# Causal masks of two query tiles as matmuls, VectorE's program as a loop, and side jobs in other steps: a cross-attention and expert-layer kernel

## The chip, the cores and the metric

The kernel runs on one core of a Trainium2 chip. The metric is the device time of one execution in microseconds (us), here the median of the runs shown; lower is better. The engines are TensorE (PE in profile rows; its weight loads are PEld), VectorE (DVE), ScalarE (ACT), GpSimd (POOL) and SyncE (SP), which issues most of the DMAs.

## The reference, cut to what matters

For 16 batches of 512 tokens with 256 features: 16-head attention (head size 16) against 1601 context tokens under a causal mask, then a layer in which 8 experts each pick 128 tokens of a batch.

```python
q = x @ Wq.T ; k = context @ Wk.T ; v = context @ Wv.T        # 16 heads of 16
scores = einsum('bhqd,bhkd->bhqk', q, k) * SCALE
causal = tril(ones((t, kv_t)))                                 # key <= query
scores = where(causal, scores, -inf)
probs = softmax(scores, axis=-1)
y = einsum('bhqk,bhkd->bhqd', probs, v) @ Wo.T + bo
x = x + tanh(g_xattn) * y
...
gating, idx = top_k(softmax(layernorm(x) @ gate_w.T), k)       # per expert, 128 of 512 tokens
x = x + tanh(g_ffn) * scatter_add(gating * (silu(h @ w_gate) * (h @ w_up)) @ w_down)
```

Because of the mask only the first 512 context tokens matter. A softmax row needs the maximum over the keys at or before its query, so the mask must act before the maximum is taken.

## The kernel before, in words

The kernel has two stages, `attention` and `experts`, one after the other. The change touches `attention` alone, and in it the part that runs once for each of the 16 batches.

**Steps.** The order of all work of a batch is written out by `steps(b)` (before: lines 81 to 126) and every engine's program walks the same list, taking from it what is its own. The list has 4 groups (of 4 heads) by 11 units `k`. Each of the 44 steps has a `("max", b, g, k)` piece, then, for `k < 10`, a `("sc", ...)` piece, then the side jobs that the table `extra[g][k]` puts there. A step is named (g, k) below.

**max.** `MAX_UNITS` cuts a group's 4 heads and 4 query tiles of 128 into 11 units: unit 0 is query tile 0 of four heads (4 matmuls of 128 columns), units 1 and 2 are tile 1 of two heads each (2 matmuls of 256 columns), units 3 to 6 are tile 2 and units 7 to 10 tile 3 of one head each (one matmul of 384 or 512 columns). A query tile needs only the keys up to its own, so a head's tiles have 128, 256, 384 and 512 columns. TensorE (line 453) writes the unresolved scores into one of three PSUM banks, up to two units ahead of VectorE (semaphore `max_read`). VectorE (line 681) then runs, for every head of the unit, one custom instruction that adds the mask tile `causal` and takes the row maximum, and reads the accumulator into `mx`. Its throw-away output goes to `masked`.

**sc.** TensorE computes the scores again, transposed and with minus the maximum added (lines 470 and 473; the fp32-accurate product is made from stacked bf16 parts), into one of two banks; ScalarE takes the exponential (line 565) and frees the bank (`exp_done`); GpSimd zeroes the masked diagonal blocks of `prob` (line 834).

**Side jobs.** `pv` multiplies probabilities with values (line 487, fp32, one piece for each key tile j, 4 a group) and ScalarE's `pv+` takes the result out; `yt`, `yt+` turn and normalise it; `mt`, `mt+` turn the maxima into a row (`m_sb`) and `mrow` sends it into the stacked operand `qs`; `q`, `k`, `v`, `o` are the projections (`q` and `k` are 12 matmuls of 512 columns each a batch, `v` and `o` 24 of 256 each), with `q+`, `k+`, `v+`, `o+` taking them out; `ln1`, `ln2` are layer-norm statistics on VectorE and `ln1+`, `ln2+` their application on ScalarE; `xt`, `ll`, `lt` make the expert logits; `xsplit`, `csplit`, `ysplit`, `xs` are bf16 splits on GpSimd; `qstore`, `kstore`, `qstack`, `kstack`, `xturn`, `cturn`, `yturn`, `load`, `res`, `save`, `mrow` are DMAs that SyncE issues in the list's order. Jobs that need a PSUM bank alternate between two (`JOB_BANK`). Side jobs belong to neighbouring batches (b - 2 to b + 2), so the stage is a software pipeline.

**Programs.** TensorE, ScalarE, GpSimd and SyncE run `rounds`: batches -1 to 2 written out, 3 to 13 as a hardware loop whose semaphore targets come from registers, 14 to 17 written out. VectorE runs `rounds_apart`, in which all 19 rounds are written out with constant targets:

```python
    def rounds_apart(body):
        for b in range(-1, BATCH + 2):
            for p in steps(b):
                body(b, p)
```

`wait_apart(eng, s, value, passed)` is a wait that, where its value is a register, is followed by an increment of the semaphore `passed`, so that it stays an instruction of its own.

Of the kernel before, what the change touches and what calls it, by code (L numbers as in the profile page):

```python
# [5 lines left out]
ALU = mybir.AluOpType  # L6
# [73 lines left out]
def steps(body):  # L80
# [7 lines left out]
        0: {0: [("pv", b - 1, 1, 0)],  # L88
            1: [("yt", b - 1, 0), ("pv", b - 1, 1, 1)],
            2: [("yt+", b - 1, 0), ("ln1+", b + 1, 0)],  # L90
            3: [("pv", b - 1, 1, 2), ("mrow", b - 1, 3), ("xsplit", b + 1, 0)],
            4: [("mt+", b - 1, 3), ("mt", b - 1, 3), ("ln1+", b + 1, 1)],
            5: [("pv", b - 1, 1, 3), ("o+", b - 2, 0), ("o", b - 2, 0, 0), ("o", b - 2, 0, 1), ("xsplit", b + 1, 1)],
            6: [("pv+", b - 1, 1), ("csplit", b + 1, 0), ("csplit", b + 1, 1)],
            7: [("o", b - 2, 1, 0), ("o", b - 2, 1, 1), ("o+", b - 2, 1), ("xturn", b + 1)],
            10: [("yt", b - 1, 1), ("qstack", b, 2), ("kstack", b, 2), ("cturn", b + 1)]},
        1: {1: [("mt", b, 0)], 2: [("yt+", b - 1, 1)],
            3: [("pv", b - 1, 2, 0), ("mt+", b, 0), ("ln2", b - 2, 0), ("ysplit", b - 1, 0)],
            4: [("q", b + 1, 0, 0), ("q", b + 1, 0, 1), ("q+", b + 1, 0)],
            5: [("pv", b - 1, 2, 1), ("ln2", b - 2, 1)],  # L100
            6: [("yturn", b - 1, 0), ("q", b + 1, 1, 0), ("q", b + 1, 1, 1), ("q+", b + 1, 1)],
            7: [("pv", b - 1, 2, 2)], 8: [("mrow", b, 0)],
            9: [("pv", b - 1, 2, 3), ("xs", b - 2), ("ln2+", b - 2, 1)],
            10: [("pv+", b - 1, 2), ("ln2+", b - 2, 0)]},
# [79 lines left out]
def attention(nc, ctx, stack, sb, sem, g):  # L184
# [103 lines left out]
    def rounds(eng, body):  # L288
# [7 lines left out]
        for b in range(BATCH - 2, BATCH + 2):  # L296
            for p in steps(b):
                body(b, p)

    def rounds_apart(body):  # L300

        for b in range(-1, BATCH + 2):
# [944 lines left out]
```

## Time and profile before

| | |
|---|---|
| runs | 1906.61, 1907.35, 1908.03 us; median 1907.35 us |
| profiled execution | 1905.62 us, of which the span from first to last instruction is 1903.9 us |
| busy, share of the span | PE 93%, PEld 53%, DVE 57%, ACT 49%, POOL 49% |
| instructions | 40685, of them PE 12902 matmuls, DVE 3480 busy ones |
| DMA | 247.85 MB, mean 130 GB/s |

Attention takes about the first 845 us. Between 120 and 720 us every 50 us look alike. The matmul durations of the profile are those of pipelined instructions: one lasts from its start until its result is out, and the next starts long before that. What a matmul costs TensorE in a stream is therefore the distance from its start to the next start, not its duration. Register, branch, semaphore and DMA-issuing instructions are not counted as busy.

### The profile page before, as it was taken

To read this page: it belongs to the slowest core of one execution; us is meant where nothing else is said; L and a number is where in the kernel's file an instruction comes from. 1 tells how busy PE (TensorE), PEld (TensorE's weight loads), DVE (VectorE), ACT (ScalarE), POOL (GpSimd) and SP (SyncE) were. 2 spreads that over 40 slices of the span, in tenths; PEclk is the share of its full clock that TensorE was granted. 3 is DMA by queue.
4 is the path that set the end of the run, shared out by engine and by line. 5 is a ranking of instruction groups with operands and counts; after the bars stand their busy time and mean duration, and the time that the engine had idled before them with its cause. 6 is when DMAs were issued, how large, how long until landed. Compare 5 with 4: busy or idle time off the path is not lost.

```text
span 1903.9 us, 40685 instructions
## 1 busy us (share of the span) xinstructions
PE 1772.4 (93%) x12902; PEld 1017.8 (53%) x12902; DVE 1079.0 (57%) x3480; ACT 930.5 (49%) x1812; POOL 931.3 (49%) x1026
## 2 busy tenths in 40 slices
PE   3899999999999999935899999999899999999997
PEld 1355555555555555422465656565556565656565
DVE  2778888888888887737634343434343434343431
ACT  2466666666666666632334343434343434343332
POOL 6477777777777776543333232333322323333322
PEclk8899999999999999967999999999999999999999
DMA  5777777777777787347464644556736555555222
GB/s 161 163 172 188 189 188 188 188 188 188 188 188 188 188 189 168 81 132 177 100 132 84 120 98 89 98 90 122 123 61 121 100 89 98 89 97 82 48 34 23
DMA packets 408333, 247.85 MB, mean 130 GB/s; under 512 B 289303, under 2 KB 389759, under 8 KB 408191
## 3 DMA queue, kind: packets, MB, share of 16 engines
q1 hardware_dynamic: 383183, 212.39, 47.7%
q0 software_dynamic: 24576, 33.57, 11.3%
q8 instruction: 72, 1.18, 0.3%
q14 instruction: 70, 0.57, 0.1%
q10 hardware_dynamic: 432, 0.13, 0.0%
HBM read 118.63 MB, written 58.72 MB: 93 GB/s over the span
## 4 chain that ended last, share of the span: by engine, by line
PE 50%; DVE 3%; DMA 1%; issue 1%; ACT 0%; POOL 0%; SPq 0%; POOLq 0%; DVEq 0%
PE bank L1101 11%; PE bank L1102 11%; PE bank L1103 11%; PE bank L1117 6%; PE bank L1119 6%; PE bank L1118 6%; DVE h L1219 0%; DVE h L1222 0%; DVE top_at L1169 0%; ACT h L1147 0%; DVE work L1172 0%; DVE top L1167 0%; DMA rows<-tokens,row_now 0%; DMA out<-y,row_now 0%; POOL out L1067 0%
## 5 line engine op out<-in xcount | busy, mean ns | idle before, releaser
L1067 POOL DMA_INDIRECT out<-y,row_now x128 | 202.5, 1582 | 606.6 <-ACT y L1154 581.7
L681 DVE CUSTOM_DVE_ANT_0 masked<-bank,causal 128x128 bf16<-128x128 f32 (+3 forms) x1024 | 445.6, 484 | 69.1 <-PE bank L453 68.2
L565 ACT ACTIVATE prob<-bank 128x512 f32<-128x512 f32 x640 | 367.6, 596 | 158.1 <-PE bank L473 86.1
L1219 DVE TENSOR_TENSOR h<-bank,silu 128x512 f32<-128x512 f32 x256 | 176.4, 689 | 393.5 <-PE bank L1103 259.8
L1147 ACT ACTIVATE h<-h 128x512 bf16<-128x512 f32 x256 | 161.2, 630 | 345.4 <-DVE h L1219 328.5
L1117 PE MATMUL bank<-downT,h 128*128 128x256 bf16 x1024 | 279.1, 273 | 0.0
L1119 PE MATMUL bank<-downT,h 128*128 128x256 bf16 x1024 | 279.1, 273 | 0.0
L1118 PE MATMUL bank<-downT,h 128*128 128x256 bf16 x1024 | 279.1, 273 | 0.0
L1222 DVE TENSOR_TENSOR h<-h 128x512 bf16<-128x512 f32 x256 | 177.3, 692 | 179.7 <-ACT h L1147 175.5
L453 PE MATMUL bank<-ks,qs 96*128 96x128 bf16 (+3 forms) x1024 | 257.8, 306 | 21.0 <-DMA ks<-k_parts 11.4
L1101 PE MATMUL bank<-tokT,gateT 128*128 128x512 bf16 x512 | 195.0, 381 | 35.7 <-DMA tokT<-rows 28.9
L470 PE MATMUL bank<-qs,ks 128*128 128x128 bf16 x1024 | 199.8, 221 | 12.8 <-ACT prob L565 11.5
L1101 PE MATMUL bank<-tokT,upT 128*128 128x512 bf16 x512 | 194.4, 380 | 6.7 <-DVE h L1219 6.6
L487 PE MATMUL bank<-prob,v_aug 128*32 128x512 f32 (+3 forms) x2048 | 193.1, 449 | 4.5 <-ACT yT L573 2.4
L473 PE MATMUL bank<-qs,ks 98*128 98x384 bf16 (+2 forms) x768 | 196.5, 273 | 0.0
L1103 PE MATMUL bank<-tokT,gateT 128*128 128x512 bf16 x512 | 195.1, 381 | 0.0
L1102 PE MATMUL bank<-tokT,gateT 128*128 128x512 bf16 x512 | 195.1, 381 | 0.0
L1102 PE MATMUL bank<-tokT,upT 128*128 128x512 bf16 x512 | 194.3, 380 | 0.0
L1103 PE MATMUL bank<-tokT,upT 128*128 128x512 bf16 x512 | 194.2, 379 | 0.0
L834 POOL TENSOR_SCALAR_AFFINE_SELECT prob<-prob 128x512 f32<-128x512 f32 x256 | 155.9, 635 | 72.8 <-ACT prob L565 72.7
L1154 ACT ACTIVATE y<-bank,gate_now 128x256 f32<-128x256 f32 x128 | 53.8, 471 | 260.1 <-PE bank L1119 260.1
L453 PEld LDWEIGHTS bank<-ks,qs 96*128 96x128 bf16 x1024 | 86.1, 98 | 168.1 <-DVE mx L681 80.3
(141 smaller groups left out, 2702.7 us busy)
## 6 DMA issues: line engine op xcount, KB each, us to landing
q_parts<-q_sb SPq DMA_DIRECT2D x64, 192.0 KB, 2.9
k_parts<-k_sb SPq DMA_DIRECT2D x64, 192.0 KB, 3.8
qs<-q_parts SPq DMA_DIRECT2D x64, 192.0 KB, 3.0
ks<-k_parts SPq DMA_DIRECT2D x64, 192.0 KB, 3.2
x_t<-in_x SPq DMA_DIRECT2D x16, 512.0 KB, 4.2
ctx_t<-in_ctx SPq DMA_DIRECT2D x16, 512.0 KB, 4.9
qs<-q_parts SPq DMA_DIRECT2D x64, 128.0 KB, 2.9
ks<-k_parts SPq DMA_DIRECT2D x64, 128.0 KB, 3.2
```

Of the source, the lines that this page charges most:

```text
L453: last = nc.tensor.matmul(dst[:, h * w:(h + 1) * w], qs[0:STACK, gr, h0 + h, i * P:(i + 1) * P], ks[0:STACK, gr, h0 + h, 0:w], start=True, ...
L470: last = nc.tensor.matmul(dst[:, at:at + P], ks[:, gr, h0 + h, j * P:(j + 1) * P], qs[:, gr, h0 + h, j * P:(j + 1) * P], start=True, stop= ...
L473: last = nc.tensor.matmul(dst[:, at + P:at + PWIDTH[j]], ks[0:ROWS, gr, h0 + h, j * P:(j + 1) * P], qs[0:ROWS, gr, h0 + h, (j + 1) * P:T], ...
L565: nc.scalar.activation(prob[:, gr % 2, h0:h0 + nh, POFF[tiles[0]]:POFF[tiles[0]] + w], sc_bank[SC_BANK[k]][:, 0:nh * w].rearrange("p (h w) ...
L681: last = nc.vector.tensor_tensor_reduce(masked[:, (gr * NMAX + k) % 2, part], max_bank[max_at(gr, k)][:, part], causal[:, T - w:T], 1.0, L ...
L1067: nc.gpsimd.indirect_dma_start(out_rows, bass.IndirectOffsetOnAxis(ap=row_now[:, par, c, s:s + 1], axis=0), y[:, c % 2, s, :], None, compu ...
L1101: nc.tensor.matmul(banks[it % 2][:, :], hi, xh, start=(dh == 0), stop=False)
L1102: nc.tensor.matmul(banks[it % 2][:, :], hi, xl, start=False, stop=False)
L1103: last = nc.tensor.matmul(banks[it % 2][:, :], lo, xh, start=False, stop=(dh == NH2 - 1))
L1117: nc.tensor.matmul(to, hh, wh, start=(it == 0), stop=False)
L1118: nc.tensor.matmul(to, hh, wl, start=False, stop=False)
L1119: last = nc.tensor.matmul(to, hl, wh, start=False, stop=(it == IT - 1))
```

## The change

Three things change in `attention`.

1. For units 0, 1 and 2 of each group (those with more than one head), each head's score matmul is followed by a second one that adds the mask to its last 128 columns, in the same accumulation: bf16 identity `identb` against the constant `mask_qk`. VectorE then takes the maxima of the whole unit with one plain `tensor_reduce` over a full bank, in place of 4 (unit 0) or 2 (units 1, 2) custom instructions with their accumulator reads. Units 3 to 10 stay as they were.
2. VectorE runs the same `rounds` as the other engines: batches 3 to 13 as a hardware loop.
3. The table `extra` is another one: the same 100-odd side jobs, in other steps and in another order within a step.

`identb` is cast once by VectorE; `mask_qk` is made once by GpSimd with a memset and an `affine_select` ahead of the others.

```diff
     extra = {
-        0: {0: [("pv", b - 1, 1, 0)],
-            1: [("yt", b - 1, 0), ("pv", b - 1, 1, 1)],
...
+        0: {0: [("mrow", b - 1, 3)],
+            1: [("ln1+", b + 1, 0), ("yt+", b - 1, 0), ("pv", b - 1, 1, 0), ("yt", b - 1, 0)],
...
@@ TensorE
                     for h in range(nh):
                         last = nc.tensor.matmul(
                             dst[:, h * w:(h + 1) * w], qs[0:STACK, gr, h0 + h, i * P:(i + 1) * P],
-                            ks[0:STACK, gr, h0 + h, 0:w], start=True, stop=True)
+                            ks[0:STACK, gr, h0 + h, 0:w], start=True, stop=nh == 1)
+                        if nh > 1:
+                            last = nc.tensor.matmul(dst[:, h * w + w - P:(h + 1) * w], identb[:, :], mask_qk[:, :],
+                                                    start=False, stop=True)
                     last.then_inc(max_filled, 1)
@@ VectorE
-                    wait(dve, max_read, n - 1)
-                    wait_apart(dve, max_filled, n + 1, passed["dve"])
-                    for h in range(nh):
-                        part = slice(h * w, (h + 1) * w)
-                        last = nc.vector.tensor_tensor_reduce(
-                            masked[:, (gr * NMAX + k) % 2, part], max_bank[max_at(gr, k)][:, part], causal[:, T - w:T], 1.0, LOWEST,
-                            ALU.add, ALU.max, mx[:, gr % 2, h0 + h, i:i + 1])
-                    last.then_inc(max_read, 1)
+                    if nh == 1:
+
+                        wait(dve, max_read, n - 1)
+                        wait_apart(dve, max_filled, n + 1, passed["dve"])
+                        nc.vector.tensor_tensor_reduce(
+                            masked[:, k % 2, 0:w], max_bank[max_at(gr, k)][:, 0:w], causal[:, T - w:T], 1.0, LOWEST,
+                            ALU.add, ALU.max, mx[:, gr % 2, h0, i:i + 1]).then_inc(max_read, 1)
+                        return
+                    wait(dve, max_filled, n + 1)
+                    nc.vector.tensor_reduce(mx[:, gr % 2, h0:h0 + nh, i], max_bank[max_at(gr, k)][
+                        :, 0:nh * w].rearrange("p (h w) -> p h w", h=nh), AX.X, ALU.max).then_inc(max_read, 1)
@@
-            rounds_apart(piece)
+            rounds(dve, piece)
@@ GpSimd, once
+            nc.gpsimd.memset(mask_qk[:, :], 0.0).then_inc(consts, 1)
...
+            nc.gpsimd.affine_select(out=mask_qk[:, :], in_=mask_qk[:, :], compare_op=ALU.is_ge, fill=NEG,
+                                    base=0, pattern=[[-1, P]], channel_multiplier=1).then_inc(consts, 1)
```

**TensorE, the first two units of a group.** First before, from a group's unit 0 to the second `sc` piece (L453 is a `max` matmul, L470 and L473 are `sc`):

```order
L453 MATMUL bank<-ks,qs 128x128 [waits max_read,stack_loaded3]
L453 MATMUL bank<-ks,qs 128x128 x3
L470 MATMUL bank<-qs,ks 128x128 [waits exp_done,mrow_loaded1]
L473 MATMUL bank<-qs,ks 128x384
L453 MATMUL bank<-ks,qs 128x256 [waits max_read]
L453 MATMUL bank<-ks,qs 128x256
L470 MATMUL bank<-qs,ks 128x128 [waits exp_done]
```

Now (L456 is the `max` matmul, L460 the mask's, L476 and L479 are `sc`), from the last head of unit 0 on:

```order
L456 MATMUL bank<-ks,qs 128x128
L460 MATMUL bank<-mask_qk,identb 128x128
L476 MATMUL bank<-qs,ks 128x128 [waits exp_done,mrow_loaded1]
L479 MATMUL bank<-qs,ks 128x384
L456 MATMUL bank<-ks,qs 128x256 [waits max_read]
L460 MATMUL bank<-mask_qk,identb 128x128
L456 MATMUL bank<-ks,qs 128x256
L460 MATMUL bank<-mask_qk,identb 128x128
L476 MATMUL bank<-qs,ks 128x128 [waits exp_done]
```

Each head of units 0 to 2 has its mask matmul behind it: 4 + 2 + 2 = 8 a group, 32 a batch, 512 in all, and each stands in front of the signal `max_filled`.

**VectorE, units 1 to 3 of a group.** Before, in the program written out, units 1 and 2 with the `yt+` behind them and unit 3:

```order
L681 ISA masked,mx<-bank,causal 128x256 [waits max_filled,max_read]
L681 ISA mx 128x1
L681 ISA masked,mx<-bank,causal 128x256
...
L704 RECIPROCAL rden<-bank 128x16 [waits yt_filled]
L708 TENSOR_TENSOR yq<-bank,rden 128x4x64 [waits y_lo_split,rden_done]
L681 ISA masked,mx<-bank,causal 128x384 [waits max_filled,max_read]
```

Now, in the loop's body (REGISTER_ALU and the ISA rows of L152 compute a semaphore target in a register), units 0 to 3:

```order
L152 ISA [waits mt_filled]
L692 TENSOR_REDUCE mx<-bank 128x4 [waits max_filled]
L152 REGISTER_ALU
L692 TENSOR_REDUCE mx<-bank 128x2 [waits max_filled]
L152 ISA
L713 RECIPROCAL rden<-bank 128x16 [waits yt_filled]
L152 ISA [waits rden_done]
L717 TENSOR_TENSOR yq<-bank,rden 128x4x64 [waits y_lo_split]
L152 REGISTER_ALU
L692 TENSOR_REDUCE mx<-bank 128x2 [waits max_filled]
L152 REGISTER_ALU [waits max_read]
L687 ISA masked,mx<-bank,causal 128x384 [waits max_filled]
```

Three reduces stand where eight custom instructions and eight accumulator reads stood; every wait of the loop has a register instruction before it; `yt+` of group 0 has moved from step (0, 2) to (0, 1).

**TensorE, two `pv` pieces side by side.** Before, `pv` of key tile 1 of group 1 stands in step (0, 1) and that of tile 2 in step (0, 3). Now both stand in step (0, 3), behind `mt` (L501), with only a register instruction between them:

```order
L152 ISA [waits v_read]
L501 MATMUL bank<-ident,mx 16x128 [waits max_read]
L152 REGISTER_ALU
L493 MATMUL bank<-prob,v_aug 32x384 [waits zeroed]
L493 MATMUL bank<-prob,v_aug 32x384 x3
L152 REGISTER_ALU
L493 MATMUL bank<-prob,v_aug 32x256 [waits zeroed]
```

The same happens with tiles 2 and 3 of group 0 in step (3, 10).

## Rows read from the trace of the kernel before

**Rows 1.** The page: busy time of the engines, and TensorE's granted clock in 40 slices.

```profile
PE 1772.4 (93%) x12902; PEld 1017.8 (53%) x12902; DVE 1079.0 (57%) x3480; ACT 930.5 (49%) x1812; POOL 931.3 (49%) x1026
PEclk8899999999999999967999999999999999999999
```

**Rows 2.** Busy time by window: us, each engine (instructions), clock, DMA share, GB/s.

```profile
219.00:696.30 477.30, 465.13 (x4211) 256.30 (x4210) 392.62 (x1691) 330.42 (x660) 363.00 (x461) 1.00 0.74 189
```

**Rows 3.** Timeline of PE, 365 to 376 us: start, duration, line, what, [idle before].

```profile
365.63 0.38 PE L453 MATMUL bank<-ks,qs 96*128 96x512 bf16 x1
365.84 0.22 PE L470 MATMUL bank<-qs,ks 128*128 128x128 bf16 x1
365.90 0.27 PE L473 MATMUL bank<-qs,ks 98*128 98x256 bf16 x1
...
370.05 1.06 PE L487 MATMUL bank<-prob,v_aug 128*32 128x512 f32 x8
371.05 0.39 PE L453 MATMUL bank<-ks,qs 96*128 96x256 bf16 x2
371.28 0.22 PE L470 MATMUL bank<-qs,ks 128*128 128x128 bf16 x1
...
373.62 0.22 PE L470 MATMUL bank<-qs,ks 128*128 128x128 bf16 x1
373.77 0.64 PE L487 MATMUL bank<-prob,v_aug 128*32 128x256 f32 x8
...
374.86 0.33 PE L453 MATMUL bank<-ks,qs 96*128 96x384 bf16 x1
375.60 0.23 PE L470 MATMUL bank<-qs,ks 128*128 128x128 bf16 x1 [0.41 <-ACT prob L565]
```

**Rows 4.** What PE and its weight loads waited for, 219 to 696 us: total, times, longest.

```profile
PEld bank L453 <- DVE mx L681: 44.6, 99, 0.8
PEld bank L470 <- ACT prob L565: 15.3, 30, 0.7
```

**Rows 5.** Groups of VectorE by form, 219 to 696 us: busy, mean ns | idle before.

```profile
L681 DVE CUSTOM_DVE_ANT_0 masked<-bank,causal 128x512 bf16<-128x512 f32 x160 | 103.1, 685 | 5.6 <-PE bank L453 5.2
L681 DVE CUSTOM_DVE_ANT_0 masked<-bank,causal 128x384 bf16<-128x384 f32 x161 | 85.9, 547 | 24.3 <-PE bank L453 24.2
L681 DVE CUSTOM_DVE_ANT_0 masked<-bank,causal 128x128 bf16<-128x128 f32 x160 | 36.8, 285 | 0.0
L733 DVE TENSOR_REDUCE lmax<-bank 128x4 f32<-128x32 f32 x10 | 1.9, 186 | 0.0
```

**Rows 6.** Timeline of DVE, 366 to 373 us.

```profile
366.75 0.69 DVE L681 CUSTOM_DVE_ANT_0 masked<-bank,causal 128x512 bf16<-128x512 f32 x1
367.37 0.08 DVE L681 DVE_READ_ACCUMULATOR2_ANT mx<- 128x1 f32 x1
...
371.22 0.29 DVE L681 CUSTOM_DVE_ANT_0 masked<-bank,causal 128x128 bf16<-128x128 f32 x1
371.44 0.08 DVE L681 DVE_READ_ACCUMULATOR2_ANT mx<- 128x1 f32 x1
...
372.07 0.42 DVE L681 CUSTOM_DVE_ANT_0 masked<-bank,causal 128x256 bf16<-128x256 f32 x1
372.42 0.08 DVE L681 DVE_READ_ACCUMULATOR2_ANT mx<- 128x1 f32 x1
```

**Rows 7.** Timeline of ACT at the end of its loop's body.

```profile
369.31 0.60 ACT L573 ACTIVATE yT<-bank 128x512 f32<-128x512 f32 x1
370.00 0.60 ACT L565 ACTIVATE prob<-bank 128x512 f32<-128x512 f32 x1
```

**Rows 8.** Timeline of POOL in the prologue.

```profile
0.81 0.20 POOL L845 MEMSET ident<- 128x128 f32 x1 [0.29 <-POOLq L1237]
4.17 0.28 POOL L854 TENSOR_SCALAR_AFFINE_SELECT ident<-ident 128x128 f32<-128x128 f32 x1
```

**Rows 9.** Busy time by window behind the end of attention.

```profile
845.00:860.00 15.00, 0.80 (x4) 0.39 (x2) 13.68 (x27) 7.85 (x13) 9.11 (x11) 0.50 0.84 251
```

More of the change, by code:

```diff
@@ new lines, in steps @@
+        1: {0: [("qstack", b, 2), ("kstack", b, 2)],
+            1: [("yturn", b - 1, 0), ("yt+", b - 1, 1), ("mrow", b, 0), ("ysplit", b - 1, 0)],
+            2: [("mt", b, 0), ("mt+", b, 0), ("ln2", b - 2, 0)],
+            3: [("ln2", b - 2, 1), ("pv", b - 1, 2, 0), ("q", b + 1, 0, 0)],
+            4: [("q+", b + 1, 0), ("q", b + 1, 0, 1), ("q", b + 1, 1, 0)],
+            5: [("pv", b - 1, 2, 1)],
+            6: [("q", b + 1, 1, 1), ("kstack", b, 3), ("q+", b + 1, 1)],
+            8: [("k", b + 1, 0, 0), ("ln2+", b - 2, 1), ("pv", b - 1, 2, 2)],
+            9: [("xs", b - 2), ("ln2+", b - 2, 0), ("pv", b - 1, 2, 3)]},
@@ new lines, in steps @@
+        2: {1: [("pv+", b - 1, 2), ("k+", b + 1, 0), ("k", b + 1, 0, 1)],
+            2: [("mt", b, 1), ("mt+", b, 1)],
+            3: [("load", b + 2), ("pv", b - 1, 3, 0)],
+            4: [("k", b + 1, 1, 0), ("k", b + 1, 1, 1), ("k+", b + 1, 1)],
+            5: [("qstack", b, 3), ("yt", b - 1, 2), ("yt+", b - 1, 2), ("pv", b - 1, 3, 1)],
+            7: [("pv", b - 1, 3, 2), ("qstore", b + 1), ("vaug", b)],
+            8: [("pv+", b - 1, 3), ("mrow", b, 1), ("pv", b - 1, 3, 3), ("xt", b - 2, 0), ("xt+", b - 2, 0)],
+            9: [("res", b - 1), ("xt+", b - 2, 1)],
+            10: [("xt", b - 2, 1)]},
@@ new lines, in steps @@
+        3: {0: [("kstore", b + 1)],
+            1: [("mt+", b, 2), ("yt", b - 1, 3), ("yt+", b - 1, 3), ("qstack", b + 1, 0), ("mt", b, 2)],
+            3: [("ll+", b - 2), ("pv", b, 0, 0), ("ll", b - 2), ("v", b + 1, 0, 0), ("kstack", b + 1, 0)],
+            4: [("v+", b + 1, 0), ("v", b + 1, 0, 1), ("ln1", b + 2, 0), ("mrow", b, 2)],
+            5: [("ysplit", b - 1, 1), ("save", b - 2), ("lt", b - 2), ("yturn", b - 1, 1)],
+            6: [("kstack", b + 1, 1), ("v", b + 1, 1, 0), ("lt+", b - 2)],
+            8: [("v", b + 1, 1, 1), ("pv", b, 0, 1), ("v+", b + 1, 1)],
+            9: [("pv+", b, 0)],
+            10: [("ln1", b + 2, 1), ("pv", b, 0, 2), ("qstack", b + 1, 1), ("pv", b, 0, 3)]},
@@ L173, in flamingo @@
         ident = sb(stack, "ident", [P, P], F32)
+        identb = sb(stack, "identb", [P, P], BF16)
         aff = sb(stack, "aff", [P, NT, BATCH * EXPERTS], F32)
@@ L296, in rounds @@
         for b in range(BATCH - 2, BATCH + 2):
[L297 to L302, printed above, removed]
             for p in steps(b):
@@ L434, in _ @@
             pe.wait_ge(evac, n + 1)
+            pe.wait_ge(cast, 1)
             def piece(body, p):
@@ L750, in _ @@
             dve.wait_ge(consts, CONSTS)
+            nc.vector.tensor_copy(identb[:, :], ident[:, :]).then_inc(cast, 1)
             piece(-1, ("ln1", 0, 0))
```

48 lines of the change are left out of this document (14 added, 34 removed).

## The prediction

> **What bounds the kernel now.** I read the page first: TensorE is busy 93% of the span, all others near half, and its clock stands at the full level, 2.4 GHz, in nearly every slice [rows 1]. The change touches attention alone, so the windows come next. Over 219 to 696 us VectorE is busy for 392.6 of 477.3 us (82%), ScalarE for 69%, GpSimd for 76% and TensorE for 97% [rows 2]. By the code ScalarE has 66 instructions a batch (40 exponentials, 26 in side jobs); 660 of them stand in that window, so it holds ten batches of 47.73 us, at full clock.
>
> The 97% says little, since pipelined durations overlap. I therefore count TensorE's time from start to start [rows 3]: a 512-column matmul is followed after 0.21 us, two of 256 columns take 0.23 us, a 128-column one is followed after 0.06 us. With the code's counts for a batch (40 bf16 matmuls of 512 columns at 0.215, 32 of 384 at 0.165, 80 of 256 at 0.11, 96 of 128 at 0.058) the bf16 work is 8.6 + 5.3 + 8.8 + 5.6 = 28.3 us. A `pv` piece over 512 columns takes 1.00 us, of which some 0.1 does not shrink with its columns; a group's four take about 2.7. The `sc` matmul ahead of a `pv` holds TensorE for 0.15 us where its like holds it for 0.06 [rows 3], so 0.09 goes for entering one. Sixteen pieces: 4 x 2.7 + 16 x 0.09 = 12.3 us. The fp32 transposes (29 at 0.11) and `ll` are 3.8 us. Together TensorE needs **44.5 us of the 47.73**; the other **3.2 us a batch are waits**. One such wait: the 384-column matmul at 374.86 us is followed only after 0.74 us, 0.57 more than it needs, because of ScalarE [rows 3]. The waits of weight loads say who is late: VectorE for 44.6 us in ten batches, ScalarE for 15.3 [rows 4]. Most of that hides behind the matmul still streaming, but it names VectorE as the first partner. TensorE is thus close to being the bound and is held up a little, mostly by VectorE; VectorE in turn waits for TensorE, 24.3 us in ten batches before units 3 to 6 [rows 5]. The two take turns.
>
> **The change part by part.**
>
> *Mask matmuls, added on TensorE.* 512 of 128 columns. In a dense stream one costs 0.053 us (0.21 for 512 columns) to 0.06 us (each after another kind of row, as here) [rows 3]; I take 0.058, since the mask too alternates with a matmul of another shape. That is 32 x 0.058 = 1.86 us a batch, 29.7 us in all; bounds 27 and 31. The Trainium skill, "TensorE: Matmul & The Clock Gate", section Back-to-back issue gap, gives about 81 ns for each pair of weight load and 128-column matmul in a sustained stream; by it the masks would cost 41 us. Here each `sc` matmul has its weight load too and follows after 0.06 us, so the row decides. What falls away on TensorE: twice a batch two `pv` pieces now stand side by side, which saves the 0.09 in and about as much out: 0.37 us a batch, bounds 0 and 0.4. TensorE's need becomes 44.5 + 1.86 - 0.37 = **46.0 us a batch**. This is a floor below which no order can go, and the old waits decide on which side of 47.73 the sum comes out: **break-even is at 1.7 us of waits a batch**.
>
> *Maxima, cheaper on VectorE.* The custom instruction starts again after 0.22 us for 128 columns, 0.35 for 256 and 0.62 for 512 [rows 6]. Unit 0 cost 4 x 0.22 = 0.88, units 1 and 2 2 x 0.35 = 0.70 each: 2.28 us a group. A `tensor_reduce` over 512 columns stands in no row. From below, the slope between 128 and 512 columns (685 - 285 over 384 [rows 5]) gives 0.53 us for 512 columns (a reduce of 32 columns takes 186 ns in all); from above stands the custom instruction's whole 0.685. I take its start distance, 0.62, because it reads the same full bank. 2.28 - 3 x 0.62 = 0.42 us a group, **1.7 us a batch** (bounds 0.9 and 2.8). VectorE was at 39.3 us a batch, so this is worth time only where TensorE waited for it. But the mask also delays its own unit's signal, by 0.23 us in unit 0 and 0.12 in units 1 and 2, exactly where VectorE was behind.
>
> *VectorE's loop.* The waits of the body have register instructions ahead of them, some 60 a batch by the order of the program. Where VectorE is computing they run beside it; where it was already waiting they add their time. No row prices one on VectorE. Lower bound nothing. Upper bound: ScalarE's end of loop, with a branch and register work, where the next exponential starts 0.69 us after an instruction of 0.60 [rows 7], so 0.1 us for several of them; were each of the 32 custom instructions of units 3 to 10 0.1 us later, VectorE would have 3.2 us more a batch. I take 0.5 us, near the lower end, since between two custom instructions the second starts when the first ends [rows 6] and there is 0.5 us of cover. Ten returns to the loop's head add 0.1 us each on VectorE, hidden behind units that TensorE has ahead. The shorter instruction stream saves nothing: in the steady window VectorE shows no idle time but behind other engines.
>
> *Side jobs, spread anew.* The work is the same. By durations from the same window I added up each step's VectorE and ScalarE work. The old table has `ln1+` in steps (0, 2) and (0, 4) with little TensorE work beside it, and `ln2+` in (1, 9) and (1, 10); the new one puts 2 us of TensorE work beside `ln1+` (steps (0, 1) and (0, 3)). It splits `v` and `ll` (3.3 us of TensorE in step (3, 4)) over two steps. `k+` now shares its step with `k`. That is better balanced for ScalarE, the second partner. Against it, `mt` and `mt+` of group 0 now fall into one step, so VectorE waits in order through TensorE's transpose and ScalarE's copy, with `ln2` behind it. On SyncE `mrow` of group 3 stands four steps earlier, in (0, 0), and holds that queue until `mt+` in (0, 4); behind it stands `xturn`, first needed in step (1, 3), ten steps on, so it costs nothing. `pv+` of group 0 stands one step earlier, behind a wait for `pv` of tile 3 that ScalarE would have had anyway.
>
> *Waits after the change.* Of 3.2 us a batch I put half on VectorE's side in units 0 to 2 and half on ScalarE's. The lighter maxima take away 0.8 net of the later signal, the table another 0.3, the loop gives back 0.4. I take **2.7 us**, bounds 1.0 (all but the stalls of ScalarE's bursts gone) and 3.5 (nothing absorbed, loop in full view).
>
> *Once.* GpSimd's memset and `affine_select` are 0.20 and 0.28 us [rows 8] ahead of the chain to the first batch: 0.5 us more. VectorE's cast of `identb` is about as long and hidden behind the weights' load. Behind attention TensorE is almost idle, at half clock (845 to 860 us [rows 9]); nothing there is changed.
>
> **The sum.** 46.0 + 2.7 = 48.7 against 47.73 a batch in the middle; with the first and last batches only partly overlapped, where waits and not TensorE's work set the pace, I count 12 of 16 batches in full: 12 x 0.97 + 0.5 = 12.1 us. Against the profiled execution's 1905.6 us that is 1917.7 us; the median of the runs lies 1.7 us higher, at 1907.35, so I forecast **1919 us**. A measurement of this kernel can tell about 0.2%, 3.8 us, from no change.
>
> **The rivals.**
> *The new order wins.* The lighter VectorE stays ahead in units 0 to 2 of every group, TensorE becomes the only bound, and its waits fall below 1.7 us a batch. For it speaks that VectorE was late at 99 weight loads in ten batches [rows 4], that its work falls by as much as TensorE's rises, and that the steps are better balanced. Against it: TensorE has little slack left, and a stall of ScalarE as at 374.86 us does not care about VectorE. At waits of 1.0 us the batch takes 47.0: 16 x -0.73 + 0.5 = -11.2 us, **1896 us**. It decides from waits under 1.7 us.
> *The masks at full price and the loop on top.* If TensorE waited for ScalarE and for data rather than for VectorE, nothing is absorbed, and VectorE in its loop falls behind in units 7 to 10, where it has 0.61 us of work against TensorE's 0.44 a unit. Waits of 3.5 us give 49.5: 16 x 1.77 + 0.5 = 29 us, **1936 us**. The wait at 374.86 us is for it; VectorE's idle time before the 384-column units, 24.3 us in ten batches [rows 5], is against it.
> *It evens out.* 1.8 us of waits leave 47.8 us a batch: 16 x 0.07 + 0.5 = 1.6 us more, **1909 us**. This is also the case in which the reduce is not cheaper than two custom instructions, but the table makes up for it.
>
> **Chances.** Forecast (1911 to 1927) 0.37; masks at full price (above 1927) 0.24; even (1904 to 1911) 0.13; new order wins 0.26. Slower by over 0.2% is 0.61, within it 0.13, faster 0.26. The range leaves out about a tenth at each end: it goes from 1895, at the first rival's value, to 1938, just past the second's.
>
> **What the profile will show.** Right, if a batch takes 48.2 to 49 us, with 32 more matmuls of 128 columns at a start distance near 0.058 us, VectorE's reduce near 0.6 us, and weight loads of `max` waiting for VectorE clearly less than 4.5 us a batch. The size of the masks is wrong if the distance is over 0.07 us. The first rival is seen in a batch under 47.7 us with hardly a gap between matmuls; the second in gaps as large as before and in VectorE instructions that start over 0.1 us after the one ahead, with nothing named as their cause. The forecast as a whole would be wrong if time moved outside the sixteen batches, say in the idle stretch behind attention.

## The result, and the profile after

The changed kernel takes **1885.78 us** (median of 4 runs, 1881.99 to 1887.77) against 1907.69 us (4 runs): a ratio of 0.9886, 95% interval 0.9872 to 0.9901. It is 1.1% faster. I had forecast 1919 us, slower, and the measured time lies below the whole range of 1895 to 1938 us. The profiled execution took 1881.99 us, its span 1880.3 us, 23.6 us less than before.

The page of the changed kernel, busy time and granted clock, to be laid beside [rows 1]:

```profile
PE 1763.1 (94%) x13350; PEld 1056.6 (56%) x13414; DVE 1053.8 (56%) x2649; ACT 935.4 (50%) x1812; POOL 933.9 (50%) x1028
PEclk8899999999999999959999999999999999999999
```

TensorE has 448 matmuls more on record (of 512 added; some records are missing) and yet less busy time. The clock is what it was. So TensorE did more work in less time, and busy time did not tell how much of its old time was waiting.

The copies of `llT` on ScalarE, one a batch, mark the pace; first before, then after:

```profile
L614 ACT ACTIVATE llT<-bank x16: 277/278/279, 171.2 to 841.8; 128x128 f32<-128x128 f32 x16
```

```profile
L620 ACT ACTIVATE llT<-bank x16: 277/278/278, 169.4 to 816.2; 128x128 f32<-128x128 f32 x16
```

Up to the last one attention is 25.6 us shorter; the rest of the span is 2.0 us longer (1062.1 to 1064.1 us). All of the gain is in attention, where the change was made.

Busy time by window, the changed kernel's row that answers to [rows 2]. It has 594 ScalarE instructions, hence nine batches:

```profile
262.80:676.10 413.30, 413.30 (x4078) 251.80 (x4077) 338.35 (x1053) 300.48 (x594) 325.46 (x413) 1.00 0.77 194
```

413.3 / 9 = **45.92 us a batch** against 47.73 (46.00 over ten batches, 216.1 to 676.1 us). TensorE's busy time now is the whole window. VectorE fell from 39.3 to 37.6 us a batch: 1.7 us, the figure of the prediction.

What weight loads waited for in that window, in answer to [rows 4]:

```profile
PEld bank L456 <- DVE mx L687: 24.2, 54, 0.6
PEld bank L476 <- ACT prob L571: 1.4, 9, 0.2
```

Per batch, VectorE's side fell from 4.5 to 2.7 us and ScalarE's from 1.5 to 0.16 us. Neither is TensorE's lost time itself, as a weight load can wait while the matmul ahead still streams, but the second, ScalarE's, is one that I had hardly priced. The matmuls themselves have no row at all for waits in this window.

VectorE by form, in answer to [rows 5]:

```profile
L687 DVE CUSTOM_DVE_ANT_0 masked<-bank,causal 128x512 bf16<-128x512 f32 x144 | 95.7, 688 | 11.5 <-PE bank L456 8.1
L687 DVE CUSTOM_DVE_ANT_0 masked<-bank,causal 128x384 bf16<-128x384 f32 x144 | 76.4, 548 | 16.4 <-PE bank L456 15.6
L692 DVE TENSOR_REDUCE mx<-bank 128x2 f32<-128x512 f32 x72 | 49.1, 682 | 0.0
L692 DVE TENSOR_REDUCE mx<-bank 128x4 f32<-128x512 f32 x36 | 24.8, 689 | 3.6 <-issue 3.6
```

A reduce over 512 columns takes 682 to 689 ns, like a custom instruction over as many. Before units 7 to 10 VectorE now waits 0.9 us a batch for TensorE's bank (it was 0.5), before units 3 to 6 1.7 us (it was 2.4). These rows alone do not tell who is ahead in units 0 to 2; the distances below do.

TensorE's timeline in the steady part (start, duration, line, what). A mask between two score matmuls, then, 3 us on, two `pv` pieces side by side:

```profile
408.05 0.22 PE L456 MATMUL bank<-ks,qs 96*128 96x128 bf16 x1
408.11 0.22 PE L460 MATMUL bank<-mask_qk,identb 128*128 128x128 bf16 x1
408.17 0.22 PE L476 MATMUL bank<-qs,ks 128*128 128x128 bf16 x1
...
411.49 0.27 PE L501 MATMUL bank<-ident,mx 128*16 128x128 f32 x1
411.69 1.28 PE L493 MATMUL bank<-prob,v_aug 128*32 128x384 f32 x16
412.90 0.34 PE L456 MATMUL bank<-ks,qs 96*128 96x384 bf16 x1
```

A mask holds TensorE for 0.06 us (0.058 at the median), as assumed. The two `pv` pieces (384 and 256 columns, 16 matmuls) hold it for 1.21 us together.

VectorE's timeline there:

```profile
409.25 0.17 DVE L668 TENSOR_SCALAR ln_ve<-ln_mv 128x4 f32<-128x4 f32 x1
409.82 1.29 DVE L692 TENSOR_REDUCE mx<-bank 128x4 f32<-128x512 f32 x2 [0.40 <-issue]
411.02 0.25 DVE L713 RECIPROCAL rden<-bank 128x16 f32<-128x16 f32 x1
```

The two reduces start at 409.82 and the next instruction 1.20 us later: 0.60 us each, against the 0.62 assumed. The 0.40 us "issue" is the loop's head: a branch, after which VectorE starts again, here 274 ns behind the branch, where 0.1 us had been assumed. Once a batch, it is hidden.

**Waits by start distances.** As in the prediction, I took every matmul's distance to the next start and took off what its columns need, here the distance that a matmul of this shape, with this kind of matmul behind it, shows when it is not held up (a `pv` piece counts as one). Before, waits are about 3.6 us a batch; after, about **0.4 us**, of which only 0.1 us stand in places that are late by more than 0.015 us. TensorE's need is thus 44.2 us a batch before and 45.5 after. The largest before: 0.58 at `sc` behind `max` of unit 5 in group 0 (this is the wait at 374.86 us of [rows 3]), 0.36 in step (3, 2), 0.35 ahead of group 2's unit 0, 0.29 in step (1, 2), 0.22 in (2, 2), 0.21 at `k` in (2, 4), 0.20 at `q` in (1, 4). Those behind units 0 to 2 of all groups come to about 1.5 us.

### The profile page after: what moved, and what is told of

It is laid out like the page before. It is cut to its first block, busy times and chain, and to the rows that moved or that the text cites. A ratio compares the mean times of both kernels' runs of the same rounds, so it can differ in the third digit from the quotient of the medians.

```text
span 1880.3 us, 41349 instructions
## 1 busy us (share of the span) xinstructions
PE 1763.1 (94%) x13350; PEld 1056.6 (56%) x13414; DVE 1053.8 (56%) x2649; ACT 935.4 (50%) x1812; POOL 933.9 (50%) x1028
## 4 chain that ended last, share of the span: by engine, by line
PE 51%; DVE 2%; SPq 1%; DMA 1%; issue 1%; ACT 0%; POOL 0%; POOLq 0%
PE bank L1116 11%; PE bank L1115 11%; PE bank L1117 11%; PE bank L1133 6%; PE bank L1132 6%; PE bank L1131 6%; SPq L1042 1%; DMA gate_raw<-in_L_ffn_w_gate 1%; DVE h L1233 0%; DVE h L1236 0%; ACT h L1161 0%; SPq L1021 0%; DVE top_at L1183 0%; POOL gate_nat L1060 0%; DVE work L1186 0%
## 5 line engine op out<-in xcount | busy, mean ns | idle before, releaser
L571 ACT ACTIVATE prob<-bank 128x512 f32<-128x512 f32 x640 | 361.9, 594 | 148.1 <-PE bank L479 111.4
L687 DVE CUSTOM_DVE_ANT_0 masked<-bank,causal 128x384 bf16<-128x384 f32 (+1 forms) x512 | 303.7, 618 | 55.5 <-PE bank L456 49.7
L456 PE MATMUL bank<-ks,qs 96*128 96x128 bf16 (+3 forms) x1024 | 274.7, 306 | 17.7 <-DMA ks<-k_parts 11.0
L1116 PE MATMUL bank<-tokT,gateT 128*128 128x512 bf16 x511 | 194.8, 381 | 35.9 <-DMA tokT<-rows 29.5
L476 PE MATMUL bank<-qs,ks 128*128 128x128 bf16 x1024 | 199.2, 220 | 4.8 <-DMA qs<-m_sb 2.7
L479 PE MATMUL bank<-qs,ks 98*128 98x384 bf16 (+2 forms) x768 | 196.6, 274 | 0.0
L493 PE MATMUL bank<-prob,v_aug 128*32 128x512 f32 (+3 forms) x2048 | 184.0, 443 | 2.9 <-ACT yT L579 2.9
L1115 PE MATMUL bank<-tokT,gateT 128*128 128x512 bf16 x481 | 183.1, 381 | 3.5 <-ACT silu L1155 1.9
L1117 PE MATMUL bank<-tokT,gateT 128*128 128x512 bf16 x481 | 183.3, 381 | 0.1
L1068 POOL DMA_INDIRECT rows<-tokens,row_now x128 | 130.3, 1018 | 94.7 <-DVE row_now L1224 56.7
```

Source lines behind the costliest of these rows:

```text
L456: last = nc.tensor.matmul(dst[:, h * w:(h + 1) * w], qs[0:STACK, gr, h0 + h, i * P:(i + 1) * P], ks[0:STACK, gr, h0 + h, 0:w], start=True, ...
L476: last = nc.tensor.matmul(dst[:, at:at + P], ks[:, gr, h0 + h, j * P:(j + 1) * P], qs[:, gr, h0 + h, j * P:(j + 1) * P], start=True, stop= ...
L479: last = nc.tensor.matmul(dst[:, at + P:at + PWIDTH[j]], ks[0:ROWS, gr, h0 + h, j * P:(j + 1) * P], qs[0:ROWS, gr, h0 + h, (j + 1) * P:T], ...
L571: nc.scalar.activation(prob[:, gr % 2, h0:h0 + nh, POFF[tiles[0]]:POFF[tiles[0]] + w], sc_bank[SC_BANK[k]][:, 0:nh * w].rearrange("p (h w) ...
L687: nc.vector.tensor_tensor_reduce(masked[:, k % 2, 0:w], max_bank[max_at(gr, k)][:, 0:w], causal[:, T - w:T], 1.0, LOWEST, ALU.add, ALU.max ...
L1115: nc.tensor.matmul(banks[it % 2][:, :], hi, xh, start=(dh == 0), stop=False)
```

## The experiments

The change has three parts, so the eight combinations tell what each is worth, alone and beside the others. Each cell is the median in us, and the us a batch in the steady part:

| masks of tiles 0, 1 | VectorE's program | old table | new table |
|---|---|---|---|
| VectorE | written out | 1907.7, 47.73 (before) | 1876.09, 45.30 (`newtab`) |
| VectorE | loop | 1965.31, 54.0 (`loop_only`) | 1944.16, 52.4 (`newtab_loop`) |
| TensorE | written out | 1911.12, 47.80 (`masks_oldtab`) | 1883.96, 46.03 (`after_unrolled`) |
| TensorE | loop | 1914.66, 48.09 (`masks_loop_oldtab`) | 1885.78, 45.92 (the change) |

Each ratio below is taken against times of the kernel before on the same chip; their medians lie between 1906.9 and 1908.7 us.

**The table alone** (the kernel before, with the new `extra`):

```diff
-        0: {0: [("pv", b - 1, 1, 0)],
...
+        0: {0: [("mrow", b - 1, 3)],
```

> The kernel before with nothing changed but the table of side jobs; masks on VectorE, its program written out. If the table alone took the waits away (theory T), TensorE is left with its need without masks: 45.5 - 1.86 = 43.6 us a batch plus waits under 1 us, so a batch under 44.8 us and a run near 1865 us, faster than the changed kernel. If it takes the lighter VectorE as well (theory M), waits of 2 us or more a batch remain, most of them behind VectorE in units 0 to 3 of a group: a batch of 46 us or more, a run of 1885 us or more.

Ratio to before 0.9829 (0.9813 to 0.9846): between the two theories. Its window of ten batches, and what weight loads waited for in it:

```profile
215.70:668.70 453.00, 448.04 (x4211) 261.30 (x4210) 389.70 (x1691) 331.72 (x660) 359.07 (x460) 1.00 0.79 197
```

```profile
PEld bank L459 <- DVE mx L687: 26.6, 70, 0.6
PEld bank L476 <- ACT prob L571: 3.7, 13, 0.7
```

The table takes 2.4 us a batch away, with the same instructions on every engine. Waits by start distances fall by 2.0 us, from 3.6 to 1.6; the rest, 0.46 us, is the `pv` pieces side by side. Alone, the pieces over 384 and 256 columns hold TensorE for 0.785 and 0.572 us, and side by side for 1.217, so 0.14 us goes; it goes twice a batch, and twice the 0.09 us for entering a piece. What is left of waits stands mostly in units 0 to 2: 0.35 in step (2, 0), 0.27 and 0.21 in (1, 2) and (1, 1), 0.17 in (3, 0). ScalarE's side falls from 15.3 to 3.7 us in ten batches [rows 4]. The table alone brings more than the whole change; I had credited it with 0.3 us of waits a batch.

**The masks alone** (the change, with the old table and VectorE written out):

```diff
-            rounds(dve, piece)
+            rounds_apart(piece)
```

> Masks of tiles 0 and 1 on TensorE, the old table, VectorE written out. Theory M: TensorE's waits behind VectorE fall, so the batch is at or under the 47.73 us of before, near 47 us, a run of 1893 to 1905 us. Theory T: the old table's waits stay at about 3 us and the masks come on top: 49.5 us a batch, a run near 1936 us.

Ratio 1.001 (1.0 to 1.002); one of the ten times, 3698 us, is left out of the ratio. Between the theories again, nearer to M. Window of ten batches, and waits of the weight loads:

```profile
223.30:701.30 478.00, 470.69 (x4532) 277.08 (x4530) 375.59 (x1170) 328.88 (x660) 363.49 (x462) 1.00 0.75 188
```

```profile
PEld bank L456 <- DVE mx L692: 18.8, 30, 0.8
PEld bank L456 <- DVE mx L687: 16.0, 39, 0.6
PEld bank L476 <- ACT prob L571: 9.3, 20, 0.7
```

The 32 masks are 1.86 us of matmuls a batch and cost 0.07 us. Waits fell from 3.6 to 1.8 us, those behind units 0 to 3 almost to nothing (under 0.1 us left), while the 0.58 us in (0, 5) and the 0.35 us ahead of group 2 stand as before. So the lighter VectorE absorbs nearly all of the masks, 1.8 us, where the prediction had 0.8. The wait for ScalarE in (0, 5) stays, as it had said; all that weight loads wait for ScalarE falls from 15.3 to 9.3 us in ten batches.

**Masks and loop on the old table** (the change with the old table):

> The changed kernel with the old table: masks on TensorE and VectorE's loop. Both theories expect what the run with the old table and VectorE written out shows, plus the price of the loop: under 0.3 us a batch (5 us) if register instructions hide behind the running instruction, 3 us a batch (50 us) if each of 32 custom instructions started 0.1 us later.

Ratio 1.0037 (1.0024 to 1.005).

```profile
224.20:705.10 480.90, 471.12 (x4532) 277.06 (x4531) 378.37 (x1170) 328.94 (x661) 362.40 (x461) 1.00 0.74 186
```

The loop adds 0.29 us a batch to `masks_oldtab` (0.4 had been assumed), and 0.3 us to VectorE's busy time. This kernel is slower than before by 0.4%: on the old table the masks and the loop bring nothing, and together cost a little.

**The change with VectorE written out** (edit as in `masks_oldtab`, new table kept):

> The changed kernel with VectorE's program written out. If the loop costs nothing, 1885.8 us within 2 us and 45.93 us a batch. If the loop costs something even here, faster by its price, at most the 0.4 us a batch of waits that are left (7 us).

Ratio 0.987 (0.9853 to 0.9886), overlapping that of the change.

```profile
218.90:679.20 460.30, 459.89 (x4532) 280.12 (x4531) 376.35 (x1170) 334.38 (x661) 362.19 (x462) 1.00 0.78 195
```

46.03 us a batch against 46.00: on the new table the loop costs nothing that can be measured. Against `newtab` (45.30) the masks cost 0.73 us a batch here, ten times as much as on the old table, because more than half of the waits that they could fill is gone already.

**The loop with the masks on VectorE**, on the old table and on the new:

```diff
-            rounds_apart(piece)
+            rounds(dve, piece)
```

> The kernel before with VectorE's loop alone. No price: 1907 us within 3. Full price: 50 us and more slower. My guess: 0 to 8 us slower.

> The kernel before with the new table and VectorE's loop; all masks on VectorE. Against the same with VectorE written out this is the loop's price where VectorE has the most work: 0 if register instructions hide, up to 3 to 5 us a batch (50 to 80 us) if each of the 64 custom instructions started later.

Ratios 1.0292 (1.0275 to 1.0309) and 1.0184 (1.0153 to 1.0214): 57 and 68 us lost to the loop alone. The guess for `loop_only` had been 0 to 8 us. The "full price" of 50 us and more comes close in number, but its reason, each custom instruction started later, is not the one that the trace shows. What VectorE waited for over 220 to 700 us in `loop_only`, then that kernel's window of nine batches:

```profile
DVE masked L681 <- issue: 45.4, 9, 5.3
```

```profile
222.00:708.30 486.30, 441.58 (x3790) 240.04 (x3789) 355.20 (x1522) 299.40 (x594) 327.13 (x415) 0.94 0.68 167
```

Nine times, once a batch, VectorE stands still for 5 us and waits for no one; and TensorE's clock, 1.00 in all windows above, is 0.94.

**Which masks?** To see where this begins, I masked only tile 0 on TensorE, and then only tile 1, each with the new table and the loop:

```diff
-                        if nh > 1:
+                        if i == 0:
```

```diff
-                        if nh > 1:
+                        if i == 1:
```

> The changed kernel with the mask of tile 0 alone on TensorE; units 1 and 2 are masked by VectorE's custom instructions again. TensorE has 16 masks a batch less (0.93 us), VectorE 8 x (0.70 - 0.62) = 0.6 us a batch more. If TensorE is the only bound (theory T), a batch of 45.0 us and a run near 1871 us. If VectorE's load decides (theory M), the batch stays at 45.9 or rises.

> The changed kernel with the mask of tile 1 alone on TensorE; unit 0 is four custom instructions again. TensorE has 16 masks a batch less (0.93 us), VectorE 4 x (0.88 - 0.62) = 1.0 us a batch more, in unit 0, at the head of a group. Theory T: 45.0 us a batch and 1871 us. Theory M: 46 us or more, and waits behind VectorE in units 0 to 2.

`mask_tile0` takes **1871.92 us**, ratio 0.9806 (0.9789 to 0.9823), faster than before and than the change, and near the 1871 us of theory T. `mask_tile1` takes 1976.96 us, ratio 1.0357 (1.033 to 1.0385). The window of `mask_tile0`, ten batches:

```profile
215.90:668.80 452.90, 452.64 (x4371) 269.88 (x4372) 381.96 (x1411) 331.58 (x660) 361.20 (x461) 1.00 0.78 198
```

That is 45.29 us a batch, what `newtab` takes without any mask on TensorE (45.30), and their ratios to before overlap: masking tile 0 on TensorE costs nothing, but no gain over the table alone is shown.

In `mask_tile1`, what VectorE and TensorE waited for over 220 to 700 us, then VectorE's timeline at the loop's head and TensorE's there:

```profile
DVE masked L689 <- issue: 68.8, 9, 8.8
PE bank L456 <- DVE mx L689: 65.9, 9, 8.4
```

```profile
398.31 0.17 DVE L668 TENSOR_SCALAR ln_ve<-ln_mv 128x4 f32<-128x4 f32 x1
405.80 0.29 DVE L689 CUSTOM_DVE_ANT_0 masked<-bank,causal 128x128 bf16<-128x128 f32 x1 [7.32 <-issue]
```

```profile
399.47 0.33 PE L479 MATMUL bank<-qs,ks 98*128 98x384 bf16 x1
406.79 0.50 PE L456 MATMUL bank<-ks,qs 96*128 96x384 bf16 x1 [6.99 <-DVE mx L689]
407.08 0.32 PE L476 MATMUL bank<-qs,ks 128*128 128x128 bf16 x1
```

VectorE ends an iteration at 398.5 us and starts the next at 405.8 us; TensorE, two units ahead, runs dry. Its granted clock is at half the full level, 1.2 GHz, for 7 to 10 us of each iteration behind such a stall (3 to 7 in the two kernels before). The row of `mask_tile1` for 403.6 to 410.4 us has it:

```profile
403.60:410.40 6.80, 3.61 (x22) 1.31 (x23) 3.19 (x14) 1.58 (x3) 0.80 (x2) 0.50 0.01 2
```

A 128-column matmul is followed there after 0.11 us (407.08 to 407.19) in place of 0.06. By its window of ten batches (in the last section) a batch takes 55.4 us. 7.3 us of it are TensorE's wait for VectorE (65.9 us in nine).

Counted from one branch of VectorE's loop to the next, in records of any kind, with the time from the branch to the next instruction:

| kernel | records a body | behind the branch |
|---|---|---|
| the change | 228 | 0.27 us |
| `mask_tile0` | 260 | 0.29 us |
| `mask_tile1` | 264 | 4.2 to 5.7 us |
| `loop_only`, `newtab_loop` | 296 | 4.2 to 5.2 us |

Four instructions more make the step, so either the length has a limit between 260 and 264, or the place of the body in memory decides. DMA queues in `mask_tile1`, 330 to 460 us:

```profile
q1 hardware_dynamic: 26855, 20.77, 64.5%
q14 instruction: 13, 0.11, 0.4%
q8 instruction: 1, 0.02, 0.0%
```

Instructions are being loaded in the middle of the loop; the same view of the change and of `mask_tile0` has the first row alone. To tell length from place, I put 32 one-column copies ahead of VectorE's loop and changed nothing in its body:

```diff
+            for i in range(32):
+                nc.vector.tensor_copy(pad_t[:, i:i + 1], causal[:, i:i + 1])
             rounds(dve, piece)
```

> The kernel with the mask of tile 1 alone on TensorE, with 32 small copies into an unused tile put ahead of VectorE's loop, so that the same loop body of 264 instructions lies 32 places further on in the program. If what decides is where the body lies against blocks of 256 instructions (theory A), it now touches two blocks and not three: no stall at the loop's head, no instruction transfers in the loop, about 45.3 us a batch and a run near 1873 us. If a body of 264 is simply too long (theory L), nothing changes: 1977 us.

**1879.88 us**, ratio 0.9865 (0.9842 to 0.9889): 97 us less than `mask_tile1`, with the same body of 264, and 45.75 us a batch in place of 55.4. The DMA queues over 330 to 460 us, and what VectorE waited for over 220 to 700 us:

```profile
q1 hardware_dynamic: 34502, 26.43, 78.1%
```

```profile
DVE masked L690 <- issue: 6.8, 11, 0.7
```

No instruction is loaded in the loop any more, and the branch takes 0.29 us again. That the place decides for this body is shown. Of the 9.7 us a batch between the two kernels 7.3 are TensorE's wait; the other 2.4 I put to the half clock, which was not taken apart. The Trainium skill, "Advanced Engine Details and Errata", section ISA Cache, says that the instruction memory of an engine other than TensorE holds two lines of 256 instructions; the trace agrees, in that a body which can lie across three such lines is loaded anew in each iteration, but neither the 256 nor where the lines lie does any run show. The bodies of 296 I did not move.

**Does tile 0 need the loop?** `mask_tile0` with VectorE written out:

> Mask of tile 0 alone on TensorE, VectorE's program written out. The loop's price at this load, and a candidate for the fastest version: 1868 to 1872 us, against 1871.9 with the loop. If the waits of 0.19 us a batch at unit 2 to 3 of group 1 come from register instructions, 3 us faster; otherwise the same.

1873.6 us, ratio 0.9824 (0.9807 to 0.984): as `mask_tile0`. Here too the loop neither costs nor brings anything that can be measured.

**Which moves of the table?** I took single groups of the new table into the kernel before (with the stack's loads left where the other groups need them); this is the edit for groups 1 and 2:

```diff
-        1: {1: [("mt", b, 0)], 2: [("yt+", b - 1, 1)],
...
+        1: {0: [("qstack", b, 2), ("kstack", b, 2)],
```

> The kernel before (masks on VectorE, written out) with group 0's side jobs in the steps of the new table, groups 1 to 3 as before (the stack loads of group 2 stay in group 0). The whole table gives 2.4 us a batch. Theory P (separate gains): the waits in group 0, mainly the 0.58 us in step (0, 5), go, and two pv pieces side by side save 0.3: about 0.8 us a batch, 1895 us. Theory W (only as a whole): within 4 us of 1908.

> The same with groups 1 and 2 from the new table, 0 and 3 as before. Waits of before that lie in groups 1 and 2 sum to 1.7 us a batch. Theory P: about 1.1 us a batch less, 1890 us. Theory W: within 4 us of 1908.

> The same with group 3 alone from the new table. Waits of before in group 3 sum to 0.7 us a batch. Theory P: 0.5 us for them and 0.3 for the pv pieces side by side, 1896 us. Theory W: within 4 us of 1908.

Ratios: group 0 1.0016 (1.0004 to 1.0029), groups 1 and 2 0.994 (0.992 to 0.996), group 3 0.9938 (0.9921 to 0.9954). The windows of ten batches, each kernel's own:

```profile
225.90:703.20 477.30, 463.04 (x4211) 258.32 (x4211) 393.83 (x1691) 330.81 (x660) 361.13 (x461) 1.00 0.75 188
```

```profile
220.60:686.40 465.80, 457.01 (x4212) 258.75 (x4213) 397.32 (x1689) 330.23 (x660) 358.65 (x460) 1.00 0.78 192
```

```profile
220.70:692.00 471.30, 460.31 (x4211) 254.78 (x4212) 392.71 (x1691) 330.88 (x660) 362.57 (x461) 1.00 0.77 192
```

That is 0.0, 1.15 and 0.60 us a batch, 1.75 us together, where the whole table brings 2.43. The last 0.7 us exist only with all groups. Group 3 does what theory P says, groups 1 and 2 lie between the theories. Group 0 alone brings nothing (theory W), although its largest wait goes: 0.64 us now stand at `o` in step (0, 4).

**A single move.** My explanation for the 0.58 us in (0, 5) was ScalarE, busy with `ln1+` (two instructions, 1.08 us in all) beside the exponentials. First I moved the second half one step later:

```diff
-            4: [("mt+", b - 1, 3), ("mt", b - 1, 3), ("ln1+", b + 1, 1)],
+            4: [("mt+", b - 1, 3), ("mt", b - 1, 3)],
```

and put it at the head of step (0, 5); in a second kernel the first half of `k` moved from (2, 1) to (1, 8) as well.

> The kernel before with one move: the second half of ln1+ goes from step (0, 4), where TensorE has 0.5 us of work, to step (0, 5), where it has 2.2. If single moves that put side work of ScalarE beside work of TensorE explain the table (theory P), the wait of 0.58 us a batch in step (0, 5) goes: a batch of 47.2 us, 1899 us. If the table works only as a whole (theory W), the wait turns up elsewhere and the run stays within 3 us of 1908.

> The kernel before with two moves: ln1+ as in the run before, and the first half of the k projection from step (2, 1) to step (1, 8), where VectorE had 0.61 us of work and TensorE 0.44. Theory P: the wait of 0.35 us before the maxima of group 2 goes too: 46.8 us a batch, 1893 us. Theory W: no gain over the run with one move.

Ratios 1.0018 (1.0008 to 1.0028) and 1.0054 (1.0037 to 1.0071): misses both. The wait in (0, 5) stayed at 0.58 us. In the second, the 0.35 us ahead of group 2 went and 1.32 us appeared at `sc` in (2, 2), where there had been 0.22. ScalarE's timeline of `move_ln1`:

```profile
381.63 1.08 ACT L608 ACTIVATE xn<-x_t,ln_shift,ln_rstd 128x256 f32<-128x256 f32 x2
382.61 1.07 ACT L565 ACTIVATE prob<-bank 128x512 f32<-128x512 f32 x2
```

A pair of `ln1+` lies between exponentials for 1 us. The half that made (0, 5) late had to be the first one, of (0, 2). So I moved that one a step earlier, alone:

```diff
-            2: [("yt+", b - 1, 0), ("ln1+", b + 1, 0)],
+            2: [("yt+", b - 1, 0)],
```

with `ln1+` put first among the side jobs of step (0, 1).

> The kernel before with the first half of ln1+ one step earlier, in (0, 1), where TensorE has 1.8 us of work, and not in (0, 2), where it has 0.45. If ScalarE's two copies there make it late for the exponential that TensorE waits for in step (0, 5), 0.5 us a batch less: 1900 us. If ScalarE is late because of all its side work in steps 2 to 4, within 3 us of 1908.

Ratio 0.9968 (0.9956 to 0.9981), 47.27 us a batch: the 0.5 us that had been expected. TensorE's timeline at the place of the wait at 374.86 us in [rows 3]:

```profile
373.34 0.33 PE L453 MATMUL bank<-ks,qs 96*128 96x384 bf16 x1
373.50 0.22 PE L470 MATMUL bank<-qs,ks 128*128 128x128 bf16 x1
```

0.16 us from start to start in place of 0.74. The wait is gone, and 0.46 of its 0.58 us reach the batch. One job, moved by one step, brings 0.3%; its neighbour moved by one step brings nothing.

**Each mask twice.** The changed kernel with every mask matmul issued twice (the mask is added twice, which leaves the maxima as they are):

```diff
-                        if nh > 1:
+                        for twice in range(2 if nh > 1 else 0):
```

> The changed kernel with every mask matmul issued twice (the mask is added twice, which leaves the result as it is). 512 more matmuls of 128 columns. If TensorE alone sets the pace, each costs its 0.058 us: 1.86 us a batch, 47.8 us, and 1915 us. If slack absorbs part, less; the 0.43 us a batch of waits bounds that: at least 1.4 us a batch, 1908 us.

Ratio to before 0.9982 (0.9972 to 0.9991).

```profile
219.20:696.00 476.80, 476.80 (x4852) 297.83 (x4851) 378.94 (x1170) 337.35 (x661) 362.36 (x462) 1.00 0.75 188
```

47.68 us a batch, 1.7 to 1.8 more than the change (46.00 over ten batches, 45.92 over nine) for 32 more matmuls: 0.053 to 0.055 us each. At most 0.2 of the expected 1.86 us is absorbed, so in the steady part TensorE is close to being the only bound. For the whole run the expectation missed: 1905.17 us, 19 us above the change, where 1915 and at least 1908 had been written. The ten steady batches account for 17 of the 19 us; the other six and the ends, with 192 more masks (11 us at 0.058), add some 2 us by the medians and 8 by the profiled spans. Why they cost less there was not looked into.

## Why the prediction was wrong

**Masks, 1.86 us a batch: right.** 0.058 us each at the median, 1.7 to 1.8 us a batch when doubled. By the 81 ns that the Trainium skill ("TensorE: Matmul & The Clock Gate", section Back-to-back issue gap) gives for a pair, the 32 would have been 2.6 us; the trace does not agree.

**Side-by-side `pv`, 0.37 us with bounds 0 and 0.4: a little too small.** It is 0.46 us. The sixteen pieces hold TensorE for 10.95 us a batch before and 10.46 after, but 0.2 of that difference is waiting behind two of the pieces before; the changes into two pieces give the other 0.18. TensorE's need before was 44.2 us and not 44.5, so after it is 45.5 to 45.6, where 46.0 was called a floor. That alone is 7 us of the run.

**VectorE's 1.7 us: right** (39.3 to 37.6), **the reduce at 0.62: right** (0.60).

**The loop, 0.5 us a batch on VectorE and 0.4 on the waits:** 0.29 on the old table, nothing on the new one. I had asked only what its instructions cost, and never whether its body fits in what the engine holds. Here it does, because the masks are on TensorE: with them on VectorE the loop costs 57 to 68 us where it now lies. The loop thus depends on the masks, or on luck with the place of its body, and no rival had this.

**Waits after, 2.7 us: wrong. This is the step that failed.** They are 0.4 us. Both terms that take waits away were too small. "The lighter maxima take away 0.8": alone they remove 1.8 us (`masks_oldtab`). "The table another 0.3": alone it removes 2.0 us of waits (`newtab`), 2.4 us a batch with the `pv` pieces. Together they remove 3.2 of 3.6, since some waits go with either. The table is the term that decides the sign: with the masks at their measured worth and the old table the kernel comes out no faster than before. The prediction went through the table for single jobs that could do harm, and gave the better balance a token. But 2.2 of the 3.6 us (0.58, 0.36, 0.35, 0.29, 0.22, 0.21, 0.20) sat in seven steps, each wait in one step of its own, and such waits a new table can remove. That a partner had one job too many there is shown for the first alone; four of the others (0.36, 0.29, 0.22, 0.20) go with the masks alone as well. The "stall of ScalarE as at 374.86 us does not care about VectorE" was right, and was read wrongly: it spoke against the masks alone (`masks_oldtab` keeps it), not against the change, since the table moves the very `ln1+` that causes it. `ln1_half0` shows this.

**The sum.** 45.92 in place of 48.7 a batch. Of the 2.8 us between them 2.3 are waits, 0.45 the floor. Of the 23.6 us between the spans ten batches of the steady part give 18, the six at the ends and the prologue the other 5 to 6; I had counted 12 in full, and with 16 x -1.81 the rival's formula gives -28.5 us, so 13 would have been right.

**The rivals.** "The new order wins" is what happened, by its own sign (a batch under 47.7 us, hardly a gap between matmuls), more strongly than its 1896 us: it decides from waits under 1.7 us, and had 1.0 where 0.4 came. Its reason was half right: VectorE ahead in units 0 to 2 explains why the masks cost 0.07 us a batch on the old table and 0.73 on the new one in place of 1.86, but the gain is the table's, and the change would be some 10 us faster without masks and loop (`newtab`).

What stays open: which other single moves make up the 0.7 us a batch that come only with all groups together. Only that of `ln1+` was taken apart. Nor was it tried whether a body of 296 runs without the stall in another place.

## What to carry to other kernels

When an engine is busy for 97% and still waits, list its waits by the step in which each stands: a wait that recurs in the same step may be one job too many for a partner there, and a move can take it away. The value of a hand-written order is in those few places, and the gains do not simply add up (three parts of the table, taken alone, bring 1.75 of 2.43 us); changes that fill waits and changes that remove them compete, so the masks cost 0.07 us a batch on the old table and 0.73 on the new one. When a change has several parts, run each part alone: the lowest time here, 1871.92 us (1.9% under before, 0.7% under the change), masks only tile 0 on TensorE, with the new table, and the new table with nothing else is within the noise of it (1876.09 us, ratios 0.9806 and 0.9829 with overlapping intervals).

## What the hardware showed that was not expected

A loop's body on VectorE can cost 4.2 to 5.7 us at each return where another of nearly the same length costs 0.29 us: with 264 records the run took 1976.96 us, and 1879.88 us once 32 small instructions stood ahead of the loop. In the slow case 14 packets of instructions are loaded in 130 us, in the other none. The stall costs more than itself, for TensorE goes to half clock behind it: the mean granted clock of `mask_tile1` over ten batches is 0.93 in this row of its windows, where `mask_tile0` has 1.00:

```profile
218.00:772.10 554.10, 473.68 (x4371) 275.90 (x4370) 387.59 (x1450) 336.14 (x660) 362.50 (x461) 0.93 0.65 163
```

And changing between full-width bf16 matmuls and the 32-column fp32 ones of `pv` costs TensorE 0.09 us on the way in (0.15 in place of 0.06 us behind an `sc` matmul [rows 3]) and 0.14 us on the way out, about four masks for both: two places fewer a batch saved 0.46 us.
